# An attention and FFN layer on one core: the first FFN product by seven block products, its sine argument by ScalarE and VectorE

## The reference

```
x = x + attention(layernorm(x), ctx)      # x: 8 x 1024 x 512; ctx: 8 x 64 x 384; 16 heads
h = layernorm(x) @ W1 + b1                # W1: 512 x 2048
q = h + (cos(th) * wr + sin(th) * wi) * wi * sin(th + 0.1 * h) * 0.1
x = x + relu(q) @ W2 + b2                 # W2: 2048 x 512
```

## Time and profile before

| what | value |
|---|---|
| median of 3 runs (lowest, highest) | 2029.39 us (2029.12, 2029.51) |
| span of the profiled execution, first to last instruction | 2027.3 us |
| PE busy | 2014.9 us, 99% |
| VectorE, ScalarE, POOL busy | 1342.4, 1131.6, 1021.5 us |
| HBM read, written | 98.34 MB, 68.16 MB |
| attention's end and the FFN's first matmul | about 628 and 630.33 us |

### The profile page before, as it was taken

One profiled execution on the slowest core, in us unless ns is written; L12 is line 12 of the kernel. 1 busy time (PEld: TensorE's weight loads), 2 busy tenths in 40 slices (PEclk: granted clock), 3 DMA queues, 4 the chain that ended last, 5 costly groups with the idle time before them and its releaser, 6 DMA issues.

```text
span 2027.3 us, 26664 instructions
## 1 busy us (share of the span) xinstructions
PE 2014.9 (99%) x9498; PEld 1684.9 (83%) x9498; DVE 1342.4 (66%) x1983; ACT 1131.6 (56%) x1979; POOL 1021.5 (50%) x708
## 2 busy tenths in 40 slices
PE   9999999999999999999999999999999999999999
PEld 7788888888888888888888888888888888888887
DVE  8988888888876665655555555565655555555554
ACT  6767767667665655544554454545545454554453
POOL 6877777777774453435334343433435334343521
PEclk9999999999999999999999999999999999999999
DMA  7565675655524311121111212211130211112100
GB/s 240 150 164 136 169 175 138 173 137 164 143 66 144 107 42 42 45 81 27 57 42 42 54 40 73 42 42 42 42 83 21 64 43 42 46 48 73 42 22 21
DMA packets 232822, 168.51 MB, mean 83 GB/s; under 512 B 154353, under 2 KB 184049, under 8 KB 232689
## 3 DMA queue, kind: packets, MB, share of 16 engines
q1 hardware_dynamic: 231824, 166.76, 29.8%
q10 hardware_dynamic: 864, 0.04, 0.0%
HBM read 98.34 MB, written 68.16 MB: 82 GB/s over the span
## 4 chain that ended last, share of the span: by engine, by line
PE 91%; DVE 4%; ACT 2%; POOL 1%; issue 1%; DMA 1%; SPq 0%; ACTq 0%; DVEq 0%; POOLq 0%
PE psum L1394 29%; PE psum L1396 29%; PE psum L1395 29%; PE psum L1487 2%; DVE hid L1320 1%; POOL prob L679 0%; DVE act_lo L1325 0%; POOL prob L700 0%; ACT act_hi L1001 0%; ACT hid L1012 0%; DVE top L1177 0%; DVE prob L1168 0%; DMA x_sb<-in_x 0%; DVE xt_lo L1067 0%; DVE xt_lo L1277 0%
## 5 line engine op out<-in xcount | busy, mean ns | idle before, releaser
L820 POOL TENSOR_TENSOR frac<-turns,frac 128x512 f32<-128x512 f32 x256 | 333.3, 1302 | 826.9 <-DVE frac L1350 826.9
L1320 DVE SCALAR_TENSOR_TENSOR hid<-frac,gain,hid 128x512 f32<-128x512 f32 x256 | 321.7, 1257 | 144.2 <-ACT frac L995 143.1
L1394 PE MATMUL psum<-w_hi,act_hi 128*128 128x512 f32 x1024 | 398.3, 389 | 0.0
L1395 PE MATMUL psum<-w_lo,act_hi 128*128 128x512 f32 x1024 | 398.3, 389 | 0.0
L1396 PE MATMUL psum<-w_hi,act_lo 128*128 128x512 f32 x1024 | 398.3, 389 | 0.0
L1010 ACT ACTIVATE turns<-psum,u_shift 128x512 f32<-128x512 f32 x256 | 176.5, 689 | 328.4 <-PE psum L1396 271.2
L1001 ACT ACTIVATE act_hi<-hid 128x512 fp32r<-128x512 f32 x256 | 161.8, 632 | 353.9 <-DVE hid L1320 353.9
L1325 DVE SCALAR_TENSOR_TENSOR act_lo<-hid,act_hi 128x512 fp32r<-128x512 f32 x256 | 197.6, 772 | 178.1 <-ACT act_hi L1001 178.1
L1350 DVE TENSOR_SCALAR frac<-turns 128x512 f32<-128x512 f32 x256 | 111.4, 435 | 248.1 <-ACT turns L1010 248.1
L1395 PEld LDWEIGHTS psum<-w_lo,act_hi 128*128 128x128 f32 x1024 | 192.3, 188 | 40.0
L1394 PEld LDWEIGHTS psum<-w_hi,act_hi 128*128 128x128 f32 x1024 | 192.1, 188 | 39.9
(11 more groups left out here) (149 smaller groups left out, 4013.1 us busy)
## 6 DMA issues: line engine op xcount, KB each, us to landing
res<-in_x SPq DMA_DIRECT2D x64, 256.0 KB, 3.8
x_dram<-res SPq DMA_DIRECT2D x64, 256.0 KB, 3.1
x_sb<-in_x SPq DMA_DIRECT2D x15, 1024.0 KB, 6.4
x_sb<-x_dram SPq DMA_DIRECT2D x15, 1024.0 KB, 5.5
xn<-turn_dram SPq DMA_DIRECT2D x30, 512.0 KB, 5.1
out<-x_sb SPq DMA_DIRECT2D x15, 1024.0 KB, 4.4
turn_dram<-kt SPq DMA_DIRECT2D x112, 128.0 KB, 2.4
x_sb<-turn_dram SPq DMA_DIRECT2D x28, 512.0 KB, 6.3
```

The source lines that it names most:

```text
L820: pool.tensor_tensor(frac[:, j % 2, :], turns[:, j % 2, :], frac[:, j % 2, :], ALU.subtract)\
L1320: dve.scalar_tensor_tensor(out=hid[:, j % 2, :], in0=frac[:, j % 2, :], scalar=gain[:, f:f + 1], in1=hid[:, j % 2, :], op0=ALU.mult, op1=A ...
L1394: pe.matmul(o, a_hi, b_hi, start=first, stop=False)
L1395: pe.matmul(o, a_hi, b_lo, start=False, stop=False)
```

## The change

Two tiles are now taken together, and the first FFN product is done on blocks: two blocks of 128 hidden channels, two halves of the 512 input channels, two tiles. In place of eight block products there are Strassen's seven, P1 to P7, each of 2 x 3 matmuls of 512 columns into one of four PSUM banks. A step p of a pair of tiles gives blocks 2p and 2p + 1 for both tiles; C11 and C21 belong to the first tile, C12 and C22 to the second. C11 = P1 + P2 is accumulated in its bank; the others are put together by VectorE with P1, which ScalarE copies to SBUF. The blocks of the second tile are kept (`late_hid`), and their 16 products with W2 follow at the pair's end.

The seven combinations of W1 are made during attention (28 jobs: sums by POOL, high parts by ScalarE, low parts by POOL and VectorE in turn) and go to DRAM (`w1s`), W2 during the first pair (`w2s`). From there both are brought into rings of 8 and 4 places for every pair. The seven combinations of the input (B11, B21, B22 and T1 to T4) are made by POOL, ScalarE and VectorE once a pair from tiles turned through DRAM; this now holds for the first two tiles too. The output rows are added up in buffers of their own (`acc`), loaded anew from `x1_dram`. `bo` is added to the first eight blocks of rows in attention by POOL.

For the sine, ScalarE makes `turns` and then `turns + ROUND`, and VectorE takes one operation for the (negative) fraction; POOL has no part in it.

The diff, cut to its core ("..." stands for what is left out):

```diff
+PRODUCTS = ("P1", "P6", "P4", "P2", "P5", "P7", "P3")
+NP = len(PRODUCTS)
+OPERANDS = ("B11", "B21", "B22", "T1", "T2", "T4", "T3")
+MOVING = {"P1": "B11", "P2": "B21", "P3": "B22", "P4": "T4", "P5": "T1", "P6": "T2", "P7": "T3"}
+BANK_OF = {"P1": 0, "P2": 0, "P6": 1, "P7": 1, "P5": 2, "P3": 2, "P4": 3}
+OPENS = ("P1", "P6", "P5", "P4")
...
+W1_SLOTS = 8
+W2_SLOTS = 4
...
+        def events(T):
+            order = []
+            for p in range(FP):
+                i = T * FP + p
+                order += [("product", i, name) for name in PRODUCTS[:-1]]
+                if p:
+                    order += [("second", first_half(T, 2 * p - 2), None), ("second", first_half(T, 2 * p - 1), None)]
+                order.append(("product", i, PRODUCTS[-1]))
+            order += [("second", first_half(T, FC - 2), None), ("second", first_half(T, FC - 1), None)]
+            return order + [("second", second_half(T, c), None) for c in range(FC)]
...
+            def store_job(J):
+                q, r = divmod(J, NP)
+                m = PRODUCTS.index(W1_PARTS[r])
+                job_done(sp, J)
+                sp.dma_start(w1s[2 * q:2 * q + 2, m].rearrange("g p x -> p g x"),
+                             w1_out[:, J % W1_OUTS].bitcast(F32).rearrange("p g s x -> p g (s x)"))\
+                    .then_inc(w1_stored[J % W1_OUTS], 16)
...
+                if n == TILES * NB - 2:
+                    for half in range(2):
+                        rows_out(0, half)
+                if n == TILES * NB - 1:
+                    rows_back(0)
+                    for half in range(2):
+                        rows_out(1, half)
...
+            for n in range(W1_SLOTS):
+                load_w1(n)
+            for c in range(STAGE):
+                load_w2_raw(c)
+            rows_back(1)
...
+                        if name == "P7" and p == FP - 1 and more:
+                            rows_back(2 * T + 2)
+                    else:
+                        if at + W2_SLOTS >= FC and at + W2_SLOTS < 2 * FC * FFN_PAIRS:
+                            load_w2(at + W2_SLOTS)
+                        for p, s, half in ((5, 0, 0), (6, 0, 1), (7, 1, 0)):
+                            if more and at == first_half(T, 2 * p - 1):
+                                rows_out(2 * T + 2 + s, half)
+                        if more and at == second_half(T, 1):
+                            rows_out(2 * T + 3, 1)
+                        if at == second_half(T, 1):
+                            store_acc(2 * T)
+                        if more and at == second_half(T, 3):
+                            rows_back(2 * T + 3)
+                            load_acc(2 * T + 2)
+                        if T + 2 < FFN_PAIRS and at == second_half(T, FC - 2):
+                            for s in range(2):
+                                load_rows(2 * T + 4 + s)
             for blk in range(NB):
...
+                if 0 < i + 1 - LAG_A - KC < EARLY_ROWS:
+                    bias_early_row(i + 1 - LAG_A - KC)
+                if job_at(i) is not None and job_at(i) % 2 == 0:
+                    lo_of_job(pool, job_at(i))
+                for q in range(W1_QUADS):
+                    for n in range(4):
+                        if i == job_step(NP * q + n) + 1:
+                            sum_of_blocks(q, n)
...
+            operand_sums(0, ("T1", "T2", "T4", "T3"))
...
+            def keep_p1(i):
+                act.wait_ge(prod, at_prod(i, "P1"))
+                act.wait_ge(v_done, i)
+                act.activation(p1_sb[:], psum[:, BANK_OF["P1"], :], ACT.Copy).then_inc(p1_done, 1)
...
+                act.activation(turns[:, q % 2, :], source, ACT.Identity, bias=shift, scale=0.1 / TWO_PI)\
+                    .then_inc(turns_done, 1)
+                act.wait_ge(turns_done, q + 1)
+                if q >= 2:
+                    act.wait_ge(wave_done, q - 1)
+                act.activation(frac[:, q % 2, :], turns[:, q % 2, :], ACT.Identity, bias=round_col[:])\
+                    .then_inc(whole_done, 1)
...
+                    for T in range(2):
+                        layer_stats(TILES + T, range(NB))
+                    for T in range(2):
+                        layer_shift(TILES + T)
+                if i >= STEPS_A - 2:
+                    for half in range(2):
+                        turn_late_rows(i - STEPS_A + 2, half)
...
+            def sum_v(i):
+                T, p = divmod(i, FP)
+                dve.wait_ge(prod, at_prod(i, "P7"))
+                if T:
+                    dve.wait_ge(act_lo_done, second_half(T - 1, 2 * p + 1) + 1)
+                dve.scalar_tensor_tensor(out=late_hid[:, 2 * p + 1, :], in0=psum[:, BANK_OF["P7"], :],
+                                         scalar=par[:, 3, 2 * p + 1:2 * p + 2], in1=p1_sb[:], op0=ALU.add, op1=ALU.add)\
+                    .then_inc(v_done, 1)
+            def hidden_21(i):
+                T, p = divmod(i, FP)
+                dve.wait_ge(v_done, i + 1)
+                if i:
+                    dve.wait_ge(act_lo_done, first_half(T, 2 * p - 1) + 1 if p else first_half(T - 1, FC - 1) + 1)
+                dve.tensor_tensor(hid[:, 1, :], late_hid[:, 2 * p + 1, :], psum[:, BANK_OF["P4"], :], ALU.subtract)\
+                    .then_inc(c21_done, 1)
+            def hidden_22(i):
+                p = i % FP
+                dve.wait_ge(v_done, i + 1)
+                dve.wait_ge(c21_done, i + 1)
+                rows = late_hid[:, 2 * p + 1, :]
+                dve.tensor_tensor(rows, psum[:, BANK_OF["P5"], :], rows, ALU.add).then_inc(c22_done, 1)
+            def hidden_12(i):
...
+            def fraction(q):
+                dve.wait_ge(whole_done, q + 1)
+                dve.scalar_tensor_tensor(out=frac[:, q % 2, :], in0=frac[:, q % 2, :], scalar=ROUND, in1=turns[:, q % 2, :],
+                                         op0=ALU.subtract, op1=ALU.subtract).then_inc(frac_done, 1)
...
+            def strassen(i, name):
+                p, n, j = i % FP, at_prod(i, name) - 1, OPERANDS.index(MOVING[name])
+                pe.wait_ge(w1_in[n % W1_SLOTS], 16 * (n // W1_SLOTS + 2))
+                if p == 0:
+                    pe.wait_ge(xo_lo_done, NP * (i // FP) + j + 1)
+                if name == "P1" and i:
+                    pe.wait_ge(hid_done, i)
+                elif name == "P6" and i:
+                    pe.wait_ge(v_done, i)
+                elif name == "P4" and i:
+                    pe.wait_ge(c21_done, i)
+                elif name == "P5" and i:
+                    pe.wait_ge(c12_done, i)
+                elif name == "P2":
+                    pe.wait_ge(p1_done, i + 1)
+                elif name == "P7":
+                    pe.wait_ge(u_done, i + 1)
+                elif name == "P3":
+                    pe.wait_ge(c22_done, i + 1)
+                w, to = w1_ring[:, n % W1_SLOTS], psum[:, BANK_OF[name], :]
+                for k in range(2):
+                    cols = slice(k * P, (k + 1) * P)
+                    m = product(to, (w[:, 0, cols], w[:, 1, cols]), (xo_hi[:, j, k, :], xo_lo[:, j, k, :]),
+                                name in OPENS and k == 0, k == 1, name not in OPENS)
+                m.then_inc(prod, 1)
...
-                    pool.wait_ge(whole_done, j + 1)
-                    pool.tensor_tensor(frac[:, j % 2, :], turns[:, j % 2, :], frac[:, j % 2, :], ALU.subtract)\
-                        .then_inc(frac_done, 1)
```

More of the change, by code:

```diff
@@ new lines, in loaded, with added, stored @@
+            def loaded(tile, rows):
+                pool.dma_start(tile, rows).then_inc(fix_in, 16)
+                fixed[0] += 1
+                pool.wait_ge(fix_in, 16 * fixed[0])
+            def added(instruction):
+                instruction.then_inc(fix_add, 1)
+                fixed[1] += 1
+                pool.wait_ge(fix_add, fixed[1])
+            def stored(rows, tile):
+                pool.dma_start(rows, tile).then_inc(fix_out, 16)
+                fixed[2] += 1
+                pool.wait_ge(fix_out, 16 * fixed[2])
@@ new lines, in uniform @@
+            def uniform(n, rows, tile, u_row, room, b):
+                loaded(tile, rows(x_rows))
+                loaded(u_row, u_dram[b].partition_broadcast(P))
+                added(pool.tensor_tensor(tile, tile, u_row.unsqueeze(1).to_broadcast([P, tile.shape[1], C]), ALU.add))
+                for blk in range(tile.shape[1]):
+                    row = tile[:, blk, :]
+                    added(pool.tensor_scalar(room, row, 0.0, None, ALU.mult))
+                    added(pool.tensor_scalar(room.bitcast(I32), room, 0.0, None, ALU.is_equal))
+                    added(pool.tensor_tensor(row.bitcast(I32), row.bitcast(I32), room.bitcast(I32), ALU.mult))
+                if n < 2:
+                    added(pool.tensor_tensor(tile, tile, bo_row[:].unsqueeze(1).to_broadcast([P, tile.shape[1], C]),
+                                             ALU.add))
+                stored(rows(x1_rows), tile)
@@ L836, in _ @@
```

(10 more changed lines are left out.)

907 lines of the change are left out of this document (557 added, 350 removed).

## The result

| | median us (lowest, highest) | ratio to before, 95% |
|---|---|---|
| before, same chip | 2029.26 (2029.07, 2029.51) | |
| changed | 2209.22 (2207.26, 2211.88) | 1.0889 [1.0873, 1.0904] |

What follows compares the result with a forecast made beforehand. The prediction took the FFN to be bound by its number of matmuls alone. It summed 2027.3 - 87 + 35 + 34 + 33 + 2 + 15 = 2059, plus 2.1, to 2061 us, range 2018 to 2093.

Steps and rivals of the forecast that it cites:

- Matmuls, -87: FFN: 720 matmuls instead of 768 per two tiles, 10.9 us less in each of eight pairs, 87 us in all.
- VectorE hidden in the FFN: Steps 2 to 7 of a pair: 15 VectorE operations at 0.6 (9 us) hidden behind 14.96 us of PE.
- P2's wait 1.0: Step 1 of a pair: P2 waits 1.0 us for ScalarE's copy of P1, queued behind the step before.
- a wave beside POOL's L820: FFN, VectorE's L1320: its 1.26 us was read as beside POOL's instruction; without POOL, 0.75 was taken.
- P3 waits: Step p = 0 of a pair: P3 waits 2.4 us for three VectorE operations in a row after P7.
- act_lo at block 15: After a pair's last P3: some 3.7 us of operations beside 2.72 us of matmul, a wait of 1.0 us.
- DMA stall, +34: Second tile's second product: block 8's weights come 4.8 us late in each of seven pairs, 34 us.
- rival 1: DMA queue not strictly in order, or the ring has slack: the 34 us go, 2027 us remain; chance 0.22.
- Start, +33: FFN's start: both tiles turned through DRAM, way back behind ten weight DMAs, P6 late by 33 us; bounds 20 and 42.
- Attention, +15: Attention: added POOL work, eight of 16 sums ahead of halves 10 us, together 15; bounds 0 and 28.
- Clock, rival 3: PE's pauses throttle the clock, 15 x 2.1 = 31 us, giving 2092; chance 0.14 together with heavier DMA.
- 2035 to 2085: Kernel time in us that the forecast's own bounds were said to give, before widening for rivals 1 and 3.

Runs made afterwards that it cites:

- e5: Changed kernel with the 1 MB load of accumulator rows issued seven blocks later, behind block 10 of the second tile's second product: 2203.0 us, ratio 1.0855.
- e9: Changed kernel with GpSimd's sums and low parts of W1 in attention cut to one column for three of four parts: 2190.1 us, ratio 1.0794.
- e18: Changed kernel with biases in 128-column pieces, later loads and operands, reordered blocks, and GpSimd's W1 work cut in two pieces: 2160.0 us, unsteady, ratio 1.0570.
- e8: Changed kernel with matmuls that compute nothing put into PE's waits (after the first P1, before P3 at p = 0, before block 8): 2207.1 us, ratio 1.0880.
- e6: Changed kernel with the first bias row in attention issued by GpSimd behind q_lo: 2207.7 us, ratio 1.0874.
- the best version: Changed kernel with biases moved, accumulator rows and operands later, way back first, first bias row later, two second-product blocks between P7 and P3: 2108.0 us, ratio 1.0392.

## Why the prediction was wrong, point by point

- **Matmuls, -87:** right. 384 fewer, and with no wait they start 0.227 apart. (The last one before starts at 2023.5; the row of the chain that I read it from, is a step 1.9 us earlier.)
- **VectorE hidden in the FFN ("15 VectorE operations at 0.6"), P2's wait 1.0:** wrong, the largest part, and the step on which the prediction failed. Beside GpSimd's bias additions these operations took 2.7 to 2.9 us, and P2 waited 4.1 to 7.1. The duration came from a row with an input in PSUM (L1192), which GpSimd doesn't disturb. The earlier trace rows showed the sign: I read L1320's 1.26 us as "a wave beside POOL's L820" and took it to vanish with GpSimd's fraction, and did not ask what the remaining, longer GpSimd instructions do to VectorE. The run without them gives 81 us back, of 148 that the forecast lacks. In the last pair, without GpSimd beside it, P3 waits 2.45 and P2 1.07, so that part of the sum was right by itself, as was act_lo at block 15 (1.1 measured, 1.0 forecast). In the six pairs between, P3 waits 2.4 to 4.0.
- **DMA stall, +34:** right in place and size: 4.2 us for 4.8, 31.1 us on the page. That it would return 34 us if removed would have been wrong (e5: 6): the turned tile's landing also starts GpSimd's sums, which hold up act_lo. The order of the queue held, so rival 1 (2027) falls.
- **Start, +33:** 40. The chain was right; GpSimd's T1 to T4 took 2.4 to 3.2 us each and not 1.91, and two of VectorE's low parts 6.5 us beside them, the same lock.
- **Attention, +15:** 44, mis-sized, and the second step that failed. 22 of GpSimd's 30 sums and low parts cost 21.5 us, the other eight about 9, since nearly each, not every second sum, moves `q_lo` or `halves` or makes VectorE late: `xt_lo` has a mean of 1297 ns, 911 before and 984 again in e9. How much of it is their place in GpSimd's list and how much the lock stays open, as e18 failed to tell. The bias rows cost some 13 us and not 4, as the first waits 7.0 us for a DMA ahead of `q_lo`; a wait was added, and what was queued behind it not followed.
- **Clock, rival 3:** it came: a granted clock of 0.93 in the window above, 43 us of matmuls at 1.2 GHz where the forecast had 2 and the rival 31. But with VectorE held up these were no price of their own: e8 took 19 us of them away and gained 2, which is less than its runs can tell. What they cost without the lock, no run shows by itself.
- **Range:** no term had the GpSimd neighbour in it. The "2035 to 2085" is also not what the stated bounds add up to: taken all at one end they give 1964 and 2141, and the measured time lies above even that.

With the measured numbers the sum closes: -87 + 44 + 40 + 129 + 43 = 169 of 178; the other 9 are steps of PE that are neither clearly a pause nor clearly slow.

## What to carry to other kernels

Before an instruction's duration is taken from a trace, look at what the neighbour did in that row: on VectorE, an operation with two SBUF inputs took 2.7 to 2.9 us beside a two-input GpSimd instruction of 2.7 us, and 0.7 without it. Work called off the critical path still has a price if it shares a lock, and the removed wait's successor has to be priced with it (e5, e6, e8: three true causes that gave back 6, 2 and 2 us). Fewer matmuls pay only as long as PE is the chain: here the FFN of the best version, with 384 matmuls fewer, still takes 5 us longer than the old one.
